# Gate weights split once and kept in HBM, norms and x scaling on ScalarE, rotary sum on GpSimd, the chunk loop written out

## The chip, the cores and the metric

The kernel runs on one core of one Trainium2 chip. The metric is the device time of one execution in microseconds (us). Five engines run their own instruction streams and meet at semaphores: TensorE (PE, its weight loads PEld), VectorE (DVE), ScalarE (ACT), GpSimd (POOL) and SyncE (SP), which here issues every DMA.

## The reference

One decoder layer on x of 2 x 1024 tokens, 256 wide, in float32:

```python
x = layernorm(x + mamba(x))       # rmsnorm, 1024-wide input projection, causal conv of 4 taps, silu,
                                  # selective scan with 16 states over 512 channels, gate, output projection
x = layernorm(x + xattn(x, ctx))  # two 8-head cross-attentions to the same 64 context tokens, rotary on
                                  # q and k, one softmax over 128 keys, W_o, layernorm, 256x256 layer, relu
x = layernorm(x + moe(x))         # 8 experts, top 2 of a softmax gate, plus a shared one; each is
                                  # (silu(x@w1+b1) * (x@w3+b3)) @ w2 + b2
# rotary: t * cos + rotate_half(t) * sin
```

The kernel computes all 9 expert networks for all tokens and weighs them. For w1 and w3 it splits weights and activations in a rounded part (hi) and a remainder (lo), so that three fast products (hi*hi, hi*lo, lo*hi) give the precision of float32.

## The kernel before, in words

**Tiling.** The 2048 tokens are four chunks of 512, two for each sequence. A chunk passes a first part, the mixer (rmsnorm, projections, conv, scan, output projection, first layernorm), and a second part (attention, layer norms, experts).

**Stages.** The second part of chunk j runs beside the mixer of chunk j+1. `body(i)` issues the mixer of chunk i and the second part of chunk i-1. body(0) has a mixer alone, bodies 1 to 3 have both and are a hardware loop (`Fori`), and body(4) has a second part alone; bodies 0 and 4 are written out already. So five stretches follow one another: a scan alone, three times scan and second part together, and a second part alone.

**What sets the order.** A list of steps written by hand, `schedule()`. Every engine walks the same list and issues its own share of each step, in order. The scan has 35 steps s; each holds, in this order: `early` work of the second part, the state sums (DVE, L1103, two), `mid` work of the second part, the scan step (DVE, L1051, two scans; ACT, L627, the two exponentials of the next step; POOL, L531, one product dbu of 128x1024 for the next step), and `late` work. dbu has a ring of three buffers, so POOL may be some steps ahead. The second part has its own counter of such steps, t = s + 2; below, "step" means one of these.

- t = 1 to 3, the rotation: q is computed on PE in four PSUM banks, ACT copies it with its bias to SBUF (L650), SP swaps neighbouring partitions by DMA, POOL multiplies the swapped copy by sin (L548, two of 128x1024), DVE multiplies by cos (L1193, two) and adds (L1198, two). PE's scores (L836) wait for both sums, and DVE's maximum of the scores (L1203) stands one step later.
- t = 14 and 15, the inner layernorm `xl`; t = 17 and 18, the layernorm `x2`. DVE makes mean and variance (`deviations`), POOL the power -0.5 of the variance (L537), DVE applies both (L1129, four of 128x256), then PE transposes. `x1` after the mixer and `xo` at the end go the same way.
- t = 20 to 39, the experts, 18 halves c. For each half SP loads 256 KB of w1 and w3 (L427), ACT rounds them to w_hi (L693), POOL makes w_lo (L555). PE multiplies (L862, six for the gate rows a and six for b), ACT makes two halves of the silu (L706, L708), POOL multiplies one by the expert's weight (L563, 16 of 18 halves), DVE multiplies them (L1219, two SBUF inputs) and takes in b (L1225, one input from PSUM), and PE applies w2 (L939). This is done for each of the four chunks, so 72 times.
- At s = 23 to 26 the next chunk is fetched: SP loads it into xn, ACT squares it, DVE and POOL make the rms, and DVE scales it (L1014, four of 128x256). The loop does so in body 3 too, for a chunk that does not exist; it loads chunk 0 again and nobody uses it.

## Time and profile before

| what | us |
|---|---|
| median of 3 runs | 1235.49 |
| the three runs | 1227.16, 1235.49, 1241.56 |
| span of the profiled execution | 1224.7 |

Apart from the span nothing is recorded of the profiled execution's own time; the three runs lie 2.5 to 16.9 us over its span.

| engine | busy us | share of the span |
|---|---|---|
| PE | 929.7 | 76% |
| PEld | 700.9 | 57% |
| DVE | 922.6 | 75% |
| POOL | 528.2 | 43% |
| ACT | 489.6 | 40% |

An average over unlike stretches says little, so the stretches are read one by one: busy time by engine in each, then the chain of waits inside it. Times in rows are us from the start of the span; L12 is line 12 of the kernel before.

### The profile page before, as it was taken

The page shows a single profiled execution, that of the slowest core. Times are in us where ns is not written, and L with a number is a line of the kernel's source. Part 1 is how long each engine was busy: PE and PEld are TensorE (multiplying, and loading weights), DVE is VectorE, ACT ScalarE, POOL GpSimd, SP SyncE. Part 2 cuts the span into 40 slices and gives each one's busy share as a digit, 9 for nine tenths or more (in the row PEclk, how much of TensorE's full clock was granted, in tenths as well). Part 3 has the DMA queues.
Part 4 walks back from the last instruction along what each step waited for, and adds up shares of the span by engine and source line. Part 5 has one row for each costly group of instructions (what it writes and reads, how often), then busy time and mean ns, then how long its engine had stood idle before and what let it go on. Part 6 is the DMA issues. An engine that isn't in the chain of part 4 may idle for free.

```text
span 1224.7 us, 13783 instructions
## 1 busy us (share of the span) xinstructions
PE 929.7 (76%) x3960; PEld 700.9 (57%) x3960; DVE 922.6 (75%) x1323; ACT 489.6 (40%) x911; POOL 528.2 (43%) x311
## 2 busy tenths in 40 slices
PE   4845549668689899577689899486789896677996
PEld 2434435256468685165477785165468683554885
DVE  2699996589999966689999965789789965322233
ACT  3534423544246434454345424454245421211442
POOL 1266540453457740533367730544257741001553
PEclk9855558778669999678679899678579997665999
DMA  5100101201023211101023211201023212000331
GB/s 193 36 35 35 52 1 35 70 35 61 18 70 121 77 45 54 70 35 61 18 78 127 73 36 55 85 18 61 18 72 119 86 35 91 21 1 9 117 109 42
DMA packets 38254, 72.61 MB, mean 59 GB/s; under 512 B 3871, under 2 KB 12712, under 8 KB 38174
## 3 DMA queue, kind: packets, MB, share of 16 engines
q1 hardware_dynamic: 38174, 71.65, 17.8%
q8 instruction: 37, 0.61, 0.2%
q14 instruction: 43, 0.35, 0.1%
HBM read 65.14 MB, written 2.30 MB: 55 GB/s over the span
## 4 chain that ended last, share of the span: by engine, by line
PE 45%; DVE 23%; issue 20%; POOL 6%; ACT 3%; DVEq 1%; POOLq 0%; DMA 0%; ACTq 0%; SPq 0%
PE ps L862 11%; DVE hs L1051 7%; PE ps L939 7%; PE ps L718 6%; PE ps L797 5%; POOL dbu L531 4%; DVE yacc L1103 4%; PE ps L836 3%; PE ps L791 2%; PE ps L825 2%; DVE work L1219 2%; PE ps L881 2%; PE ps L776 2%; DVE xn L1014 1%; POOL work L563 1%
## 5 line engine op out<-in xcount | busy, mean ns | idle before, releaser
L531 POOL TENSOR_TENSOR dbu<-v,bbc 128x1024 f32<-128x1024 f32 x128 | 308.9, 2418 | 257.3 <-DVE hs L1051 136.3
L1051 DVE TENSOR_TENSOR_SCAN hs<-ps,carry,dbu 128x512 f32<-128x512 f32 x256 | 313.3, 1266 | 10.1 <-ACT ps L627 8.2
L627 ACT ACTIVATE ps<-delta,neg_a 128x512 f32<-128x512 f32 x256 | 175.7, 692 | 300.5 <-DVE hs L1051 300.4
L718 PE MATMUL ps<-ident,hs 128*128 128x128 f32 x1024 | 189.1, 344 | 116.5 <-DVE yacc L1103 99.5
L718 PEld LDWEIGHTS ps<-ident,hs 128*128 128x128 f32 x1024 | 157.0, 180 | 150.0 <-DVE hs L1051 72.4
L1103 DVE SCALAR_TENSOR_TENSOR yacc<-ps,ctok,yacc 128x512 f32<-128x512 f32 x240 | 167.3, 737 | 1.2 <-PE ps L718 1.0
L555 POOL TENSOR_TENSOR w_lo<-w13s,w_hi 128x512 fp32r<-128x512 f32 x72 | 94.5, 1313 | 145.1 <-ACT w_hi L693 145.1
L939 PE MATMUL ps<-w2s,work 128*128 128x256 f32 x576 | 140.4, 388 | 0.3
L939 PEld LDWEIGHTS ps<-w2s,work 128*128 128x128 f32 x576 | 109.0, 196 | 15.9 <-DVE work L1225 1.5
L1219 DVE SCALAR_TENSOR_TENSOR work<-work 128x512 f32<-128x512 f32 x72 | 82.3, 1143 | 46.5 <-POOL work L563 45.6
L862 PE MATMUL ps<-x_hi,w_hi 128*128 128x512 f32 x288 | 107.9, 457 | 9.4 <-DVE work L1225 9.2
L706 ACT ACTIVATE work<-ps,half_b 128x512 f32<-128x512 f32 x72 | 49.5, 688 | 160.9 <-PE ps L862 151.3
L836 PE MATMUL ps<-kblk,work 128*128 (+1 forms) x128 | 47.5, 536 | 67.3 <-DVE work L1198 57.6
L563 POOL TENSOR_TENSOR work<-work,cbc 128x512 f32<-128x512 f32 x64 | 84.3, 1317 | 22.6 <-ACT work L706 22.6
L862 PE MATMUL ps<-x_hi,w_lo 128*128 128x512 f32 x288 | 93.6, 407 | 0.0
L862 PE MATMUL ps<-x_lo,w_hi 128*128 128x512 f32 x288 | 93.1, 406 | 0.0
L1225 DVE SCALAR_TENSOR_TENSOR work<-ps,vec,work 128x512 f32<-128x512 f32 x72 | 54.1, 751 | 46.2 <-PE ps L862 36.1
L836 PEld LDWEIGHTS ps<-kblk,work 128*128 128x128 f32 x128 | 33.2, 272 | 79.0 <-issue 62.9
L862 PEld LDWEIGHTS ps<-x_hi,w_hi 128*128 128x128 f32 x288 | 55.2, 199 | 22.8 <-DVE work L1225 12.3
L862 PEld LDWEIGHTS ps<-x_hi,w_lo 128*128 128x128 f32 x288 | 56.9, 198 | 13.2
L862 PEld LDWEIGHTS ps<-x_lo,w_hi 128*128 128x128 f32 x288 | 56.5, 196 | 13.1
L797 PE MATMUL ps<-yacc,win 128*128 128x512 f32 x128 | 57.7, 610 | 0.8 <-ACT yacc L592 0.8
(159 smaller groups left out, 1243.0 us busy)
## 6 DMA issues: line engine op xcount, KB each, us to landing
w13s<-in_w SPq DMA_DIRECT2D x72, 256.0 KB, 2.9
bbc<-brow_dram SPq DMA_DIRECT2D x32, 512.0 KB, 4.0
w2s<-in_w SPq DMA_DIRECT2D x36, 256.0 KB, 2.7
cbc<-comb_dram SPq DMA_DIRECT2D x32, 256.0 KB, 3.5
work<-work SPq DMA_DIRECT2D x16, 256.0 KB, 2.3
xn<-in_x SPq DMA_DIRECT2D x5, 512.0 KB, 5.3
xt<-in_x SPq DMA_DIRECT2D x4, 512.0 KB, 3.6
rope<-in_rope_q SPq DMA_DIRECT2D x4, 512.0 KB, 4.2
```

The costliest lines, as they stand in the source:

```text
L531: pool.tensor_tensor(dbu[:, i % DRING, :, :], v[:, 2 * h:2 * h + 2, :], bbc[:, n // 2 % 2, n % 2, :].rearrange("p (o t) -> p o t", o=1) .t ...
L555: pool.tensor_tensor(w13_lo[:, c % HRING, :, :, :].bitcast(F32R), w13s[:, c % HRING, :, :, :], w13_hi[:, c % HRING, :, :, :], ALU.subtract ...
L563: pool.tensor_tensor(gac[:, ib, :], ga[:, ib, :], cbc[:, g % CRING, :], ALU.mult).then_inc(gac_done.sem, 1)
L627: act.activation(ps[:, unit % 2, :], delta[:, q, :], ACT.Exp, scale=neg_a[:, q * NS + m:q * NS + m + 1]).then_inc(da_done.sem, 1)
L718: last = pe.transpose(ps[:, bank, t * P:(t + 1) * P], src(t), ident[:, :])
L797: last = pe.matmul(ps[:, m % Q, :], win[:, k, m * P:(m + 1) * P], xnt[:, k, :], start=(k == 0), stop=(k == KD - 1))
L836: last = pe.matmul(ps[:, 4 + b // 2, b % 2 * 2 * KEYS:(b % 2 + 1) * 2 * KEYS], qr[:, b, tile * P:(tile + 1) * P], kblk[:, bass.ds(j // CPS ...
L862: last = pe.matmul(o, left(l, k).bitcast(F32R), right(r, k).bitcast(F32R), start=(i == 0 and k == 0), stop=(i == len(terms) - 1 and k == K ...
L939: last = pe.matmul(out_cols(tile), hh[:, ib, tile * P:(tile + 1) * P], w2s[:, e % WRING, ib * DM:(ib + 1) * DM], start=False, stop=(c == 2 ...
L1051: dve.tensor_tensor_scan(hs[:, m % 2, q, 0:TC], ps[:, unit % 2, :], dbu[:, n % DRING, q % 2, :], carry[:, m, q:q + 1], ALU.mult, ALU.add). ...
L1103: dve.scalar_tensor_tensor(out=yacc[:, t, :], in0=ps[:, 2 + t % 2, :], scalar=c, in1=yacc[:, t, :], op0=ALU.mult, op1=ALU.add).then_inc(y_ ...
L1219: dve.scalar_tensor_tensor(out=gm[:, ib, :], in0=th[:, ib, :], scalar=1.0, in1=(gac if c >= 2 else ga)[:, ib, :], op0=ALU.add, op1=ALU.mul ...
```

## The change

- Gate weights. In body(0) alone, at steps s = 8 to 25, the 18 halves are staged in SBUF (SP, ring of 4, 256 KB each), rounded (ACT) and subtracted (POOL), and hi and lo are stored together in an HBM tensor (SP, 512 KB each). Each expert half of each chunk then loads hi and lo at once, 512 KB, and nothing is computed on them. The load of half c waits for the b products of half c-3; before it waited for w_lo of half c-3.
- Norms. ACT applies the four layernorms as x * rstd + shift; DVE makes -mean (128x4) and POOL shift = -mean * rstd (128x4), one small instruction each more. ACT also scales xn.
- Rotation. DVE reads q from PSUM, adds the bias and multiplies by cos in one instruction for each of 4 banks (128x512). POOL adds the two products after its two sin products.
- The loop over bodies 1 to 3 is written out, and the unused fetch in body 3 is gone.

```diff
@@ schedule
         steps += [("early", t), ("sum", s), ("mid", t), ("scan", s), ("late", t)]
+        if s >= 8:
+            steps.append(("split", s - 8))
@@ buffers
-        w13s = sb("w13s", [P, HRING, 2, KD, P])
-        w13_hi = sb("w13_hi", [P, HRING, 2, KD, P])
-        w13_lo = sb("w13_lo", [P, HRING, 2, KD, P])
+        w13x = sb("w13x", [P, HRING, 2, 2, KD, P])
+        w13_hi, w13_lo = w13x[:, :, 0, :, :, :], w13x[:, :, 1, :, :, :]
...
+        stage = work[:, 3072:5120].rearrange("p (a n) -> p a n", a=SRING)
+        w13_dram = nc.dram_tensor("w13_dram", (2 * ALL, P, 4 * KD * P), F32, kind="Internal").ap()
@@ streams
-            body(0, True, False)
-            with eng.Fori(1, CHUNKS, 1) as i:
-                body(i, False, False)
-            body(CHUNKS, False, True)
+            for i in range(CHUNKS + 1):
+                body(i, i == 0, i == CHUNKS)
@@ SP
+            def stage_half(c):
+                if c >= SRING:
+                    sp.wait_ge(lo_done.sem, c - SRING + 1)
+                sp.dma_start(stage[:, c % SRING, :], w13[c]).then_inc(stage_in[c % SRING].sem, 16)
+            def split(c):
+                if c == 0:
+                    sp.wait_ge(setup_pe.sem, 2)
+                    for k in range(SRING):
+                        stage_half(k)
+                if 1 <= c <= 2 * ALL:
+                    sp.wait_ge(lo_done.sem, c)
+                    sp.dma_start(w13_dram[c - 1], w13x[...]).then_inc(w13_out[(c - 1) % HRING].sem, 16)
+                    if c - 1 + SRING < 2 * ALL:
+                        stage_half(c - 1 + SRING)
             def load_half(j, c):
-                if c >= HRING:
-                    sp.wait_ge(*lo_done.at(j, c - HRING + 1))
-                else:
-                    sp.wait_ge(*lo_done.at(j, 0))
-                sp.dma_start(w13s[:, c % HRING, ...], w13[c]).then_inc(w13_in[c % HRING].sem, 16)
+                if j == 0 and c < HRING:
+                    for s in range(HRING):
+                        sp.wait_ge(w13_out[s].sem, 16 * (2 * ALL // HRING))
+                sp.wait_ge(*b_ps.at(j, max(0, c - HRING + 1)))
+                sp.dma_start(w13x[:, c % HRING, ...], w13_dram[c]).then_inc(w13_in[c % HRING].sem, 16)
...
-                c = t - T_EXP + 1 + HRING
+                c = t - T_EXP - 1 + HRING
                 if HRING <= c < 2 * ALL:
                     load_half(j, c)
@@ POOL
+                if kind == "split" and n < 2 * ALL:
+                    pool.wait_ge(hi_done.sem, n + 1)
+                    pool.tensor_tensor(w13_lo[:, n % HRING, ...], stage[:, n % SRING, :], w13_hi[:, n % HRING, ...],
+                                       ALU.subtract).then_inc(lo_done.sem, 1)
...
             def rstd_of(j, k):
...
+                pool.wait_ge(*norm[k]["rstd"].at(j, 1))
+                pool.tensor_tensor(shift[k][:, :], minus[k][:, :], rstd[k][:, :], ALU.mult
+                                   ).then_inc(norm[k]["shift"].sem, 1)
...
+                        for s in range(2):
+                            b = slice(2 * s, 2 * s + 2)
+                            pool.wait_ge(*sin_done.at(j, s + 1))
+                            pool.wait_ge(*cos_done.at(j, 2 * s + 2))
+                            pool.tensor_tensor(qr[:, b, :], qr[:, b, :], qs[:, b, :], ALU.add).then_inc(q_done.sem, 1)
...
-                    c = t - T_EXP + 1
-                    if 0 <= c < 2 * ALL:
-                        pool.wait_ge(*hi_done.at(j, c + 1))
-                        pool.tensor_tensor(w13_lo[:, c % HRING, ...], w13s[:, c % HRING, ...],
-                                           w13_hi[:, c % HRING, ...], ALU.subtract).then_inc(lo_done.sem, 1)
@@ ACT
+                if kind == "fetch" and n == 3:
+                    act.wait_ge(*rms_done.at(j, 1))
+                    for t in range(NT):
+                        last = act.activation(xn[:, t, :], xn[:, t, :], ACT.Copy, scale=rms[:, t:t + 1])
+                    last.then_inc(xn_done.sem, 1)
+                if kind == "split" and n < 2 * ALL:
+                    act.wait_ge(stage_in[n % SRING].sem, 16 * (n // SRING + 1))
+                    if n >= HRING:
+                        act.wait_ge(w13_out[n % HRING].sem, 16 * (n // HRING))
+                    act.activation(w13_hi[:, n % HRING, ...], stage[:, n % SRING, :], ACT.Copy).then_inc(hi_done.sem, 1)
...
+            def normalise(j, k, src, dst, after):
+                act.wait_ge(*norm[k]["shift"].at(j, 1))
+                for t in range(NT):
+                    act.activation(dst[:, t, :], src[:, t, :], ACT.Identity, scale=rstd[k][:, t:t + 1],
+                                   bias=shift[k][:, t:t + 1]).then_inc(after.sem, 1)
@@ PE
-                    pe.wait_ge(*lo_done.at(j, c + 1))
+                    pe.wait_ge(*w13_in[c % HRING].at(j, 16 * (c // HRING + 1)))
@@ DVE
                 dve.tensor_scalar(ve[k][:, :], mean[:, :, 1], EPS, None, ALU.add).then_inc(norm[k]["ve"].sem, 1)
+                dve.tensor_scalar(minus[k][:, :], mean[:, :, 0], -1.0, None, ALU.mult).then_inc(norm[k]["ve"].sem, 1)
...
                 if t == T_ROT:
-                    for s in range(2):
...
-                        dve.tensor_tensor(qr[:, b, :], qr[:, b, :], rope_part(0), ALU.mult).then_inc(cos_done.sem, 1)
-                    for s in range(2):
...
-                        dve.tensor_tensor(qr[:, b, :], qr[:, b, :], qs[:, b, :], ALU.add).then_inc(q_done.sem, 1)
+                    dve.wait_ge(*rope_in.at(j, 16))
+                    for b in range(HB):
+                        dve.wait_ge(*qs_in[b // 2].at(j, 32))
+                        dve.scalar_tensor_tensor(out=qr[:, b, :], in0=ps[:, 4 + b, :], scalar=col("bq", b),
+                                                 in1=rope[:, 0, :], op0=ALU.add, op1=ALU.mult).then_inc(cos_done.sem, 1)
```

GpSimd in body(0), at s = 8 and after. Before, 27 products dbu stand in a row:

```order
L510 MEMSET vx 128x528
L531 TENSOR_TENSOR dbu<-v,bbc 128x1024 x27
L515 TENSOR_TENSOR rms<-ms,power 128x4
L531 TENSOR_TENSOR dbu<-v,bbc 128x1024 x5
```

Now:

```order
L535 MEMSET vx 128x528
L561 TENSOR_TENSOR dbu<-v,bbc 128x1024 x10
L548 TENSOR_TENSOR w13x<-work,w13x 128x512
L561 TENSOR_TENSOR dbu<-v,bbc 128x1024
L548 TENSOR_TENSOR w13x<-work,w13x 128x512
L561 TENSOR_TENSOR dbu<-v,bbc 128x1024
```

From the tenth on, each dbu has one remainder (L548, `stage` is part of `work`) ahead of the next.

VectorE in body(1), at the rotation and the two steps after it. Before:

```order
L1193 TENSOR_TENSOR work<-work,rope 128x1024 x2
L1196 ISA
L1198 TENSOR_TENSOR work<-work 128x1024
L1196 REGISTER_ALU
L1198 TENSOR_TENSOR work<-work 128x1024
...
L1203 TENSOR_REDUCE mx<-ps 128x8
```

Now, in one piece (L1099 is the scan, L1227 the cos product):

```order
L1099 SCALAR_TENSOR_TENSOR hs<-ps,carry,dbu 128x512 x2
L1227 SCALAR_TENSOR_TENSOR work<-ps,vec,rope 128x512 x4
L1099 SCALAR_TENSOR_TENSOR hs<-ps,carry,dbu 128x512 x2
L1233 TENSOR_REDUCE mx<-ps 128x8
```

The sums have left VectorE. They stand on GpSimd now, ahead of the dbu of the third scan step (L581 is sin, L587 the sum):

```order
L561 TENSOR_TENSOR dbu<-v,bbc 128x1024 x2
L581 TENSOR_TENSOR work<-work,rope 128x1024 x2
L587 TENSOR_TENSOR work<-work 128x1024 x2
L561 TENSOR_TENSOR dbu<-v,bbc 128x1024 x11
```

## Rows read from the trace of the kernel before

**Rows 1.** Stages: us, busy us of each engine (instructions), clock share, DMA share, GB/s.
```profile
62.80:182.00 119.20, 58.25 (x240) 47.07 (x240) 119.20 (x130) 46.62 (x86) 69.14 (x30) 0.50 0.09 31
508.90:616.00 107.10, 68.41 (x345) 54.94 (x345) 101.10 (x126) 42.98 (x91) 49.05 (x22) 0.74 0.11 36
616.00:731.00 115.00, 105.64 (x507) 88.67 (x507) 102.50 (x129) 51.78 (x97) 74.10 (x47) 0.92 0.25 81
1129.60:1210.00 80.40, 79.72 (x348) 65.66 (x349) 27.53 (x59) 33.57 (x54) 41.30 (x32) 0.98 0.31 95
```

**Rows 2.** Timeline, scan alone: start us, us, engine, line, [idle before <- releaser].
```profile
95.53 1.38 DVE L1103 SCALAR_TENSOR_TENSOR yacc<-ps,ctok,yacc 128x512 f32<-128x512 f32 x2
95.65 0.69 ACT L627 ACTIVATE ps<-delta,neg_a 128x512 f32<-128x512 f32 x1 [0.48 <-DVE hs L1051]
95.76 2.35 POOL L531 TENSOR_TENSOR dbu<-v,bbc 128x1024 f32<-128x1024 f32 x1 [1.31 <-DVE hs L1051]
96.83 2.45 DVE L1051 TENSOR_TENSOR_SCAN hs<-ps,carry,dbu 128x512 f32<-128x512 f32 x2
...
99.20 1.38 DVE L1103 SCALAR_TENSOR_TENSOR yacc<-ps,ctok,yacc 128x512 f32<-128x512 f32 x2
...
157.94 5.13 DVE L1014 TENSOR_SCALAR xn<-xn,rms 128x256 f32<-128x256 f32 x4
```

**Rows 3.** Timeline, the rotation of the second overlapped stretch.
```profile
508.32 4.64 POOL L548 TENSOR_TENSOR work<-work,rope 128x1024 f32<-128x1024 f32 x2
...
511.29 6.02 DVE L1193 TENSOR_TENSOR work<-work,rope 128x1024 f32<-128x1024 f32 x2
...
517.24 4.49 DVE L1198 TENSOR_TENSOR work<-work 128x1024 f32<-128x1024 f32 x2
...
521.92 3.78 PE L836 MATMUL ps<-kblk,work 128*128 x8 [15.86 <-DVE work L1198]
```

**Rows 4.** Timeline, VectorE at the norms of that stretch.
```profile
583.13 5.01 DVE L1129 TENSOR_SCALAR xa<-xa,mv_xl,rstd_xl 128x256 f32<-128x256 f32 x4
...
596.82 0.76 DVE L1177 SCALAR_TENSOR_TENSOR x<-ps,x 128x256 f32<-128x256 f32 x2 [1.34 <-PE ps L907]
...
604.13 3.27 DVE L1129 TENSOR_SCALAR x<-x,mv_x,rstd_x 128x256 f32<-128x256 f32 x4
```

**Rows 5.** Timeline, TensorE among the experts of the first overlapped stretch.
```profile
388.69 0.81 PE L862 MATMUL ps<-x_hi,w_hi 128*128 128x512 f32 x2
...
394.04 0.81 PE L862 MATMUL ps<-x_hi,w_hi 128*128 128x512 f32 x2
```

**Rows 6.** Waits of TensorE, 385 to 415 us: us in total, times, longest.
```profile
PE ps L718 <- DVE yacc L1103: 3.4, 1, 3.4
PE ps L862 <- DVE work L1225: 3.3, 2, 1.7
```

**Rows 7.** Page, costliest groups: count | busy us, mean ns | idle before, releaser.
```profile
L555 POOL TENSOR_TENSOR w_lo<-w13s,w_hi 128x512 fp32r<-128x512 f32 x72 | 94.5, 1313 | 145.1 <-ACT w_hi L693 145.1
L1219 DVE SCALAR_TENSOR_TENSOR work<-work 128x512 f32<-128x512 f32 x72 | 82.3, 1143 | 46.5 <-POOL work L563 45.6
L1225 DVE SCALAR_TENSOR_TENSOR work<-ps,vec,work 128x512 f32<-128x512 f32 x72 | 54.1, 751 | 46.2 <-PE ps L862 36.1
```

**Rows 8.** One line each: duration ns as min/median/max.
```profile
L1219 DVE SCALAR_TENSOR_TENSOR work<-work x72: 658/693/2858, 357.2 to 1209.7; 128x512 f32<-128x512 f32 x72
```

**Rows 9.** DMA issues: count, KB each, median us from issue to landing.
```profile
bbc<-brow_dram SPq DMA_DIRECT2D x32, 512.0 KB, 4.0
...
wout<-in_w_out SPq DMA_DIRECT2D x1, 512.0 KB, 7.5
```

**Rows 10.** Stage with the most DMA traffic, columns as in rows 1.
```profile
0.00:30.00 30.00, 12.06 (x27) 6.08 (x28) 7.74 (x18) 9.47 (x21) 4.54 (x19) 1.00 0.58 197
```

**Rows 11.** Timeline of TensorE at the loop's back edge, and the tail.
```profile
464.25 1.09 PE L718 MATMUL ps<-ident,xn 128*128 128x128 f32 x8 [1.83 <-issue]
...
1099.35 1.01 POOL L537 TENSOR_TENSOR rstd_xl<-ve_xl,power 128x4 f32<-128x4 f32 x1 [56.65 <-DVE ve_xl L1123]
```

99 lines of the change are left out of this document (43 added, 56 removed).

## The prediction

> **What bounds the kernel now.** I read the busy times stage by stage first [rows 1]. In the scan alone VectorE is busy for all of 119.2 us and TensorE for half: VectorE is the bound. In the second overlapped stretch up to the experts, VectorE is busy 101.1 of 107.1 us. Among its experts TensorE is busy 105.6 of 115.0 and VectorE 102.5: the bound passes between them. The last 80 us, experts without a scan, are TensorE's alone (79.7 of 80.4). GpSimd and ScalarE are at 65% or less everywhere.
>
> Then the timeline of one scan step [rows 2]: two sums from 95.53, two scans from 96.83, the next sums at 99.20. A step is 3.67 us, 1.30 + 2.37, without a gap. One dbu of 2.35 us stands beside it on GpSimd, which then waits for its ring. Next the places where VectorE does something else: the scaling of xn [rows 2], the rotation [rows 3], the norms [rows 4], the experts [rows 5 to 8].
>
> In all of them VectorE instructions are longer than their size asks. L1219 takes 658 ns at best and 2858 at worst [rows 8], a span of one dbu. Four products of 128x256 of xn take 5.13 us [rows 2], though a scan over 128x512 takes 1.22. What suffers has all its inputs in SBUF; the sums and scans, which read PSUM, take the same time everywhere. So an instruction that leaves VectorE gives back its waiting too, where VectorE is late.
>
> **The change part by part.** The sum is made against the span, 1224.7 us; the median of the runs lies 10.8 above it, and I add that at the end.
>
> *Scaling of xn, in the scan alone:* 5.13 us leave the engine that bounds [rows 2]. ScalarE does it in four instructions of at most 0.69 (the exponential, twice as wide [rows 2]), between two exponentials that have over 1 us of slack. **-5.0**. In the other three bodies it falls among the experts, below.
>
> *The split, in the scan alone:* 18 steps get a w_hi, a w_lo, one load and one store. VectorE gets nothing, but its scans wait for dbu, which now stands behind w_lo, and that behind w_hi and the exponentials. From the end of a scan pair: exponential 0.69, w_hi at most 0.69 (same width), w_lo 1.31 [rows 7], dbu 2.35: 5.04. VectorE reaches the scan that reads this dbu after sums, a pair and sums, 4.97. So the cover is just used up: 0 to 0.1 a step, **+1**. SP stores a half one step after it is made, and w_hi needs the buffer three steps (11 us) later; its loads are issued four halves ahead. The other bound is DMA rate: 768 KB a step and the usual 512 KB in four steps are 0.92 MB. At 197 GB/s, the most this trace moves [rows 10], that is 4.7 us for a step of 3.7, +18 in all. I take +1, since the engines are only 58% busy at 197 GB/s.
>
> *Rotation, three overlapped bodies:* today two cos products 6.02 and two sums 4.49 keep VectorE from 511.3 to 521.7, and the scores start at 521.92 [rows 3]. Afterwards: four instructions of the form of L1225, 0.75 each [rows 7], done by 514.3; the sums on GpSimd run from 512.9, where the sin products end, for 2 x 2.32 (half of the 4.64 of the sin products [rows 3]), to 517.6. The scores start there. VectorE does its next scan pair meanwhile, but then stands before the maximum of the scores and waits for GpSimd and TensorE, so its own 7.5 us do not all count: -4.3, and as much in the other two, **-12.7**. The next dbu waits behind the sums, ends near 520, and its scan comes after the scores: hidden.
>
> Here a rule speaks against the change. The rows show products on GpSimd of 2.32 us beside a quiet VectorE, and VectorE's sum of the same size at 2.25 beside a busy GpSimd. The Trainium skill, GPSIMD Engine Reference, Engine selection, says to put elementwise sums of two inputs on VectorE, GpSimd being about twice as slow. The trace agrees only where VectorE is left alone. The skill's Perfetto Trace Analysis, Optimizing Scalar/DVE Operations, adds that moving work between the two "might not help" because of a shared SBUF port; that would make this term about 3 instead of 12.7, and it is rival C.
>
> *Inner norm xl, three bodies:* 5.01 us leave VectorE [rows 4]. TensorE's transposes wait for it; ScalarE has it done 1.4 us after its exponentials, some 4.2 earlier than today. VectorE already waits 1.34 us for the layer behind it at 596.8, so the gain is that of the chain: **-12.6**.
>
> *Norm x2, three bodies:* 3.27 us [rows 4], less the new small instruction and a short wait for x_hi, 2.9: **-8.7**. The norms x1 and xo stand inside the bodies where TensorE runs the projections without waiting for them: 0.
>
> *Experts, three bodies:* TensorE's step is 5.35 us where nothing holds it (394.04 - 388.69 [rows 5]). It loses 6.7 us to VectorE in the first stretch [rows 6], 6.0 and 6.7 in the others. VectorE's step without collisions is 1.30 + 2.37 + 0.66 + 0.75 = 5.08, below 5.35. With xn gone and GpSimd's load per step down from 5.0 to 3.7 us (w_lo, 72 times 1.31 [rows 7]), it should keep up. Collisions of L1219 with dbu remain possible, so I count 5.5 of each: **-16.4**. Bounds: 10.2 (only the wait behind xn, 3 x 3.4) and 19.4 (all). ScalarE's w_hi was hidden: 0.
>
> *Loads of 512 KB, 72 times:* hidden. The load of half c starts after the b products of half c-3, 2.8 us into a step, and the half is wanted two steps on: 7.9 us beside a scan, 6.2 in the tail. A 512 KB load lands in 4.0, in the crowded start in 7.5 [rows 9].
>
> *Loop:* TensorE stands 1.83 us at each of two back edges [rows 11]: **-3.7**. The unused fetch in body 3 is in the experts' term.
>
> *Tail:* four norms each get a multiplication on GpSimd and one on VectorE ahead of them, with everything waiting. No row shows the first; it lies between nothing and the power's 1.01 us [rows 11]. I take 0.3 and 0.1, as the power is most likely slow for what it computes: +1.6. The rotation there has no scan beside it; the sums are slower on GpSimd: +1.1, between -4 and +2.3. **+2.7**.
>
> Sum: -5.0 + 1 - 12.7 - 12.6 - 8.7 - 16.4 - 3.7 + 2.7 = -55.4. Span 1169.3, with 10.8 a time of **1180**.
>
> **The rivals.**
>
> A. *The expert loads become the bound (slower).* Place: every expert step. The step is at least (issue and landing + 2.8)/2. At 7.5 us of landing, 0.3 of issue, it is 5.3: hidden beside a scan, +15 in the tail. For the whole kernel to be over 12 us slower, the 54 steps at 5.35 and 18 at 4.48 must lose 67 together, a step of 6.06, so a landing of 9.0 us: about 1248. Against: 4.0 for the same size [rows 9], and 0.9 MB a step is below what 0 to 30 us moved [rows 10]. 4%.
>
> B. *The split throttles the first scan*, by DMA rate as worked out above: +17 against my term, 1197. For it: DMA traffic there rises from 31 GB/s to some 250. 12%.
>
> C. *GpSimd gives nothing back.* If its sums take 3.3 us each under VectorE's lock (6.6 for two dbu was seen), the scores come only 1 us earlier in three bodies: +9.7, 1190. This is what the second page above would have. For: GpSimd and VectorE do hold each other up. Against: the new cos products read PSUM, and such forms do not collide. 8%.
>
> D. *L1219 meets dbu in every step.* With w_lo gone GpSimd runs dbu right behind L563, and L1219 waits 2.2 us for it each time: VectorE's step is 7.3, +1.9 in some 42 steps, 1259, slower. It decides from 85% of the steps on; today the mean delay is about 0.8. A late VectorE shifts its L1219 past the dbu, so it does not lock. 2%.
>
> E. *More comes back.* VectorE is rid of some 93 us in all (60 of norms and xn, 29 of rotation, the rest collisions); if nearly the whole overlapped part is its bound, 1158. 10%.
>
> The forecast itself has 60%, with 1168 to 1193 around it for the unknown sizes; the last 4% are for mixtures of A and B that end near no change. Within 1% of 1235 (12 us) is what runs of this kernel cannot tell from none. That gives faster 0.90, same 0.04, slower 0.06. The range from **1156 to 1203** takes in the forecast, B, C and most of E, and leaves out A, D and the mixtures.
>
> **What would show it.** In the profile after: in the scan alone steps of 3.7 to 3.8 us through the split, and no stop of 5 us; dbu idle short, ended by w_lo's line. At the rotation, scores about 4 us earlier after the first scan pair, with VectorE waiting for PE ahead of the maximum. No scaling or norm rows on VectorE. Among the experts TensorE steps at 5.35 throughout and no waits for L1225 or the sums at the xn step. TensorE waiting for the w13x load would be A. L1219 near 2.8 us in the median would be D. ScalarE's norms ending later than the exponentials can bear, with scans waiting for L674, would make me wrong in a way I have priced at nothing.

## The result, and the profile after

| | median us | runs |
|---|---|---|
| before | 1238.53 | 1227.16, 1241.56, 1235.49, 1243.16 |
| changed | 1153.2 | 1155.19, 1151.21, 1150.85, 1156.8 |

The ratio is 0.9364, with a 95% interval from 0.932 to 0.9408: 85 us less. Faster was forecast at 0.90, and 1180; the time lies 27 below that and 3 below the range, next to rival E (1158). By the ratio, on the 1235.49 from which the forecast was made, it is 1156.9, at the range's lower edge. Every ratio in this document leaves out runs more than 1.5% above the quickest of their kernel, which for the kernel with the loop alone (below) are seven of ten, while the medians take in all runs. The profiled execution took 1155.19 us, its span is 1153.4, so here 1.8 lies around the span.

The engines' busy time on the page after:

```profile
PE 894.8 (78%) x3960; PEld 681.1 (59%) x3960; DVE 812.2 (70%) x1254; ACT 490.4 (43%) x929; POOL 475.0 (41%) x280
```

VectorE is rid of 110 us of work, GpSimd of 53 in spite of its new sums; ScalarE has as much as before, other things. The stages that answer [rows 1], with the same columns:

```profile
61.00:180.00 119.00, 59.01 (x244) 47.88 (x245) 117.42 (x128) 57.77 (x108) 91.04 (x48) 0.50 0.43 150
476.00:577.50 101.50, 69.07 (x349) 54.67 (x348) 86.70 (x120) 48.56 (x100) 56.74 (x28) 0.76 0.15 52
577.50:683.10 105.60, 98.53 (x503) 83.63 (x503) 89.09 (x126) 44.24 (x86) 52.46 (x29) 0.95 0.41 128
1050.00:1140.00 90.00, 88.06 (x377) 72.62 (x376) 28.65 (x62) 24.25 (x40) 20.41 (x16) 0.92 0.43 132
```

Beside the experts VectorE has gone from 102.5 of 115.0 us to 89.1 of 105.6: TensorE alone is the bound there now. Up to the experts VectorE is busy 86.7 of 101.5 us, where it was busy nearly throughout. Only the scan alone is still VectorE's.

To see where the 71 us between the spans went, I took TensorE's first instruction of each kind as a landmark and summed the way from one to the next over the three overlapped stretches. All kernels that the experiments below profiled are read with the same marks. "Gate products" are TensorE's products with w1 and w3, where the experts begin.

| us, three bodies together | before | changed | difference | forecast |
|---|---|---|---|---|
| start, to the end of the first projections | 35.9 | 34.6 | -1.2 | 0 |
| scan alone | 151.2 | 149.5 | -1.7 | -4 |
| y transposes to scores (rotation, two back edges) | 206.8 | 187.8 | -19.0 | -16.4 |
| scores to transposes of the inner norm (attention, xl) | 200.1 | 196.8 | -3.3 | -12.6 |
| those to the transposes of x2 (layer, x2) | 63.5 | 49.2 | -14.3 | -8.7 |
| those to the first gate products | 25.4 | 17.6 | -7.8 | 0 |
| gate products, first to last (experts) | 340.2 | 313.0 | -27.2 | -16.4 |
| tail, from the last gate product beside a scan to the end | 217.1 | 220.4 | +3.3 | +2.7 |

(The experts overlap the next y transposes by 7.8 us, twice, in both kernels. Less these 15.5 the rows add up to the two spans.)

**The split in the scan alone.** Timeline, with scans, exponentials, w_hi (L631), w_lo (L548) and dbu (L561); it answers [rows 2]:

```profile
93.39 2.35 POOL L561 TENSOR_TENSOR dbu<-v,bbc 128x1024 f32<-128x1024 f32 x1
...
95.05 0.62 ACT L631 ACTIVATE w13x<-work 128x512 fp32r<-128x512 f32 x1
...
95.74 1.27 POOL L548 TENSOR_TENSOR w13x<-work,w13x 128x512 fp32r<-128x512 f32 x1
95.84 2.46 DVE L1099 TENSOR_TENSOR_SCAN hs<-ps,carry,dbu 128x512 f32<-128x512 f32 x2 [0.15 <-issue]
96.97 2.35 POOL L561 TENSOR_TENSOR dbu<-v,bbc 128x1024 f32<-128x1024 f32 x1
...
99.51 2.45 DVE L1099 TENSOR_TENSOR_SCAN hs<-ps,carry,dbu 128x512 f32<-128x512 f32 x2
```

GpSimd goes dbu, w_lo, dbu without a rest, and each dbu ends (95.74, 99.32) some 0.1 to 0.2 us before the scan that reads it: a scan pair comes every 3.67 and 3.91 us by turns, 3.79 on average for 3.67 before.

**The rotation**, second overlapped stretch, answering [rows 3]:

```profile
480.38 4.65 POOL L581 TENSOR_TENSOR work<-work,rope 128x1024 f32<-128x1024 f32 x2
480.67 2.46 DVE L1099 TENSOR_TENSOR_SCAN hs<-ps,carry,dbu 128x512 f32<-128x512 f32 x2 [2.72 <-issue]
483.04 2.70 DVE L1227 SCALAR_TENSOR_TENSOR work<-ps,vec,rope 128x512 f32<-128x512 f32 x4
484.99 4.64 POOL L587 TENSOR_TENSOR work<-work 128x1024 f32<-128x1024 f32 x2
...
489.68 3.78 PE L890 MATMUL ps<-kblk,work 128*128 128x256 f32 x8 [11.83 <-POOL work L587]
493.50 1.23 DVE L1233 TENSOR_REDUCE mx<-ps 128x8 f32<-128x1024 f32 x1 [5.39 <-PE ps L890]
494.76 1.80 DVE L1236 TENSOR_SCALAR top<-mx 128x8 f32<-128x8 f32 x1
```

The scores start 9.3 us after the sin products; before, it was 13.6 (521.92 - 508.32). The new cos products take 2.70 for four, the sums 2.32 each, and VectorE waits 5.39 for TensorE ahead of the maximum, all as forecast. The last row is a thing I had not looked at: `top` has eight numbers a partition and takes 1.80 us.

**The experts**, groups of the page that answer [rows 7], and the distribution that answers [rows 8]:

```profile
L1249 DVE SCALAR_TENSOR_TENSOR work<-work 128x512 f32<-128x512 f32 x72 | 54.6, 758 | 1.2 <-ACT work L762 0.9
L1255 DVE SCALAR_TENSOR_TENSOR work<-ps,vec,work 128x512 f32<-128x512 f32 x72 | 54.1, 751 | 105.6 <-PE ps L916 85.5
```
```profile
L1249 DVE SCALAR_TENSOR_TENSOR work<-work x72: 661/682/1656, 340.7 to 1137.4; 128x512 f32<-128x512 f32 x72
```

The product gm (L1249, formerly L1219) falls from a mean of 1143 ns to 758, from a longest of 2858 to 1656, and VectorE's idle time before it from 46.5 us to 1.2. Before, 29 of the 54 gm of the three overlapped stretches began while a dbu was running; now 2 do. TensorE, which had waited 6.7 us for VectorE in 30 us [rows 6], waits for nothing at the same place (364 to 394 us).

**Loads** ([rows 9]): 512 KB of split weights land in 3.4 us, and no expert step waits for them.

```profile
w13x<-w_dram SPq DMA_DIRECT2D x72, 512.0 KB, 3.4
```

### The profile page after: what moved, and what is told of

Same layout as the page of the kernel before. It is cut to its first block, busy times and chain, and to the rows that moved or that the text cites. A ratio compares the mean times of both kernels' runs of the same rounds, so it can differ in the third digit from the quotient of the medians.

```text
span 1153.4 us, 12464 instructions
## 1 busy us (share of the span) xinstructions
PE 894.8 (78%) x3960; PEld 681.1 (59%) x3960; DVE 812.2 (70%) x1254; ACT 490.4 (43%) x929; POOL 475.0 (41%) x280
## 4 chain that ended last, share of the span: by engine, by line
PE 57%; DVE 17%; POOL 10%; issue 9%; ACT 5%; DVEq 0%; DMA 0%; POOLq 0%; ACTq 0%; SPq 0%
PE ps L916 17%; PE ps L993 10%; PE ps L772 8%; PE ps L851 5%; DVE hs L1099 5%; POOL dbu L561 5%; PE ps L890 3%; PE ps L879 3%; DVE yacc L1149 3%; POOL w13x L548 2%; PE ps L960 2%; DVE mx L1233 2%; PE ps L830 1%; ACT work L725 1%; PE ps L845 1%
## 5 line engine op out<-in xcount | busy, mean ns | idle before, releaser
L561 POOL TENSOR_TENSOR dbu<-v,bbc 128x1024 f32<-128x1024 f32 x128 | 304.1, 2385 | 213.3 <-DVE v L1085 112.3
L1099 DVE TENSOR_TENSOR_SCAN hs<-ps,carry,dbu 128x512 f32<-128x512 f32 x256 | 313.3, 1265 | 8.2 <-issue 8.0
L772 PE MATMUL ps<-ident,hs 128*128 128x128 f32 x1024 | 180.3, 333 | 93.8 <-DVE yacc L1149 78.9
L916 PE MATMUL ps<-x_hi,w13x 128*128 128x512 f32 x576 | 175.5, 428 | 0.0
L596 POOL TENSOR_TENSOR work<-work,cbc 128x512 f32<-128x512 f32 x64 | 86.7, 1355 | 203.8 <-ACT work L760 154.3
L760 ACT ACTIVATE work<-ps,half_b 128x512 f32<-128x512 f32 x72 | 49.6, 689 | 211.9 <-PE ps L916 211.9
L1255 DVE SCALAR_TENSOR_TENSOR work<-ps,vec,work 128x512 f32<-128x512 f32 x72 | 54.1, 751 | 105.6 <-PE ps L916 85.5
L916 PEld LDWEIGHTS ps<-x_hi,w13x 128*128 128x128 f32 x576 | 112.0, 197 | 24.1 <-issue 1.7
L890 PE MATMUL ps<-kblk,work 128*128 128x256 f32 x128 | 45.0, 513 | 61.3 <-POOL work L587 47.6
L916 PE MATMUL ps<-x_lo,w13x 128*128 128x512 f32 x288 | 92.2, 402 | 0.0
L916 PEld LDWEIGHTS ps<-x_lo,w13x 128*128 128x128 f32 x288 | 56.2, 195 | 12.8
L725 ACT ACTIVATE work<-ps,top 128x128 f32<-128x128 f32 x128 | 34.8, 384 | 67.4 <-DVE top L1236 67.4
L1249 DVE SCALAR_TENSOR_TENSOR work<-work 128x512 f32<-128x512 f32 x72 | 54.6, 758 | 1.2 <-ACT work L762 0.9
L1233 DVE TENSOR_REDUCE mx<-ps 128x8 f32<-128x1024 f32 x16 | 19.5, 1216 | 49.2 <-PE ps L890 49.2
L762 ACT ACTIVATE work<-ps,half_b 128x512 f32<-128x512 f32 x72 | 49.0, 681 | 0.0
```

What stands on the lines that cost most here:

```text
L561: pool.tensor_tensor(dbu[:, i % DRING, :, :], v[:, 2 * h:2 * h + 2, :], bbc[:, n // 2 % 2, n % 2, :].rearrange("p (o t) -> p o t", o=1) .t ...
L596: pool.tensor_tensor(gac[:, ib, :], ga[:, ib, :], cbc[:, g % CRING, :], ALU.mult).then_inc(gac_done.sem, 1)
L772: last = pe.transpose(ps[:, bank, t * P:(t + 1) * P], src(t), ident[:, :])
L890: last = pe.matmul(ps[:, 4 + b // 2, b % 2 * 2 * KEYS:(b % 2 + 1) * 2 * KEYS], qr[:, b, tile * P:(tile + 1) * P], kblk[:, bass.ds(j // CPS ...
L916: last = pe.matmul(o, left(l, k).bitcast(F32R), right(r, k).bitcast(F32R), start=(i == 0 and k == 0), stop=(i == len(terms) - 1 and k == K ...
L1099: dve.tensor_tensor_scan(hs[:, m % 2, q, 0:TC], ps[:, unit % 2, :], dbu[:, n % DRING, q % 2, :], carry[:, m, q:q + 1], ALU.mult, ALU.add). ...
```

## Experiments

Times are medians. Each kernel has its ratio to the kernel before on its own chip; 0.01 is 12 us. For the kernel with the loop alone I go by the ratio. The edits are shown abridged, partly in words.

| kernel | us | ratio (95%) | gm ns | top ns |
|---|---|---|---|---|
| changed | 1153.2 | 0.9364 (0.932 to 0.9408) | 758 | 973 |
| changed, weights as before | 1163.9 | 0.9467 (0.9433 to 0.9501) | 1134 | 918 |
| changed, xn on VectorE | 1167.0 | 0.948 (0.9446 to 0.9513) | 741 | 972 |
| changed, norms on VectorE | 1190.3 | 0.9679 (0.9634 to 0.9725) | 758 | 878 |
| changed, rotation as before | 1159.1 | 0.9434 (0.9397 to 0.9471) | 758 | 599 |
| changed, x2 alone on VectorE | 1163.0 | 0.9488 (0.9397 to 0.9578) | 759 | 871 |
| before, loop written out | 1223.2 | 0.9834 (0.9743 to 0.9926) | 1151 | 610 |
| before, loop written out, and the split | 1211.7 | 0.9798 (0.964 to 0.9955) | 742 | 711 |
| before, loop written out, and the norms | 1189.0 | 0.9698 (0.9627 to 0.9768) | 1144 | 508 |
| norms on VectorE, TensorE kept busy | 1193.1 | 0.9752 (0.9662 to 0.9842) | 758 | 905 |
| changed, split thinned, tail | 1146.2 | 0.9328 (0.9247 to 0.941) | 759 | 961 |
| changed, w_lo later, tail | 1142.7 | 0.9334 (0.9254 to 0.9415) | 758 | 937 |
| the last, and thinned | 1144.7 | 0.9346 (0.9272 to 0.9419) | 758 | 848 |

**1. Weights as before.** The inverse of the change's lines for the split:

```
-                steps.append(("split", s - 8))
-                sp.dma_start(w13x[...], w13_dram[c])
+                sp.dma_start(w13s[...], w13[c])
+ act:  w_hi of half c = t - T_EXP + 1, early
+ pool: w_lo of the same half, early, ahead of dbu
```

> The changed kernel with its gate weights handled as before: each chunk loads the raw half (256 KB), ScalarE makes w_hi and GpSimd w_lo in every expert step; the split in the scan alone is gone, all else is as in the changed kernel. The changed kernel lies at 1153.2 us, its expert stretches beside a scan at 104.3 each. Theory 1 (the w_lo in front of dbu is what makes dbu fall on L1249): VectorE's gm comes back to a mean of 1.0 us or more (0.76 in the changed kernel), each expert stretch to 109 to 112, the way from the x2 transposes to the first gate matmul takes some 2 us more in each body, and the scan alone becomes 2 to 4 us shorter: together +18 to +28, a time of 1171 to 1181. Theory 2 (VectorE has room now that the scaling of xn and the rest are off it, and w_lo fits): gm stays under 0.85 us, expert stretches stay within 1 us, and the time is 1150 to 1158, with nothing but the shorter scan alone to be seen.

Measured: 1163.9, +10.7, between the two theories. The mechanism is the first one's:

```profile
L1227 DVE SCALAR_TENSOR_TENSOR work<-work 128x512 f32<-128x512 f32 x72 | 81.7, 1134 | 45.7 <-POOL work L575 36.3 <-issue 8.3 <-ACT work L740 0.9
```

gm is back at 1134 ns with 45.7 us of idle time before it, and the experts take 325.9 for 313.0 (108.8, 110.2 and 106.9). Of the 54 gm beside a scan 34 begin under a running dbu again. The scan alone is 3.5 shorter, 146.0: that is the price of the split, and I had it at 1. The way from x2 to the gates did not lengthen, so that part of my first theory is wrong.

**2. Scaling of xn on VectorE.**

```
+ dve: dve.tensor_scalar(xn[:, t, :], xn[:, t, :], rms[:, t:t + 1], None, ALU.mult)
- act: act.activation(xn[:, t, :], xn[:, t, :], ACT.Copy, scale=rms[:, t:t + 1])
```

> The changed kernel with the scaling of xn back on VectorE (four products of 128x256 a chunk), all else as changed. Theory 1 (VectorE is the bound wherever a scan runs, and what stands in its row counts in full): +4 to +5 in the scan alone, +3 to +4 in each of three expert stretches, in all +13 to +17, a time of 1166 to 1170. Theory 2 (beside the experts VectorE has 0.27 us of slack a step, and the experts' step of 5.35 on TensorE absorbs one late step within the ring): +4 to +5 in the scan alone and at most 1 in each expert stretch, 1157 to 1161.

Measured: 1167.0, +13.8, in the first theory's range. 6.0 of it is in the scan alone, and 1.1, 1.9 and 2.1 in the experts, half of what I expected there; the rest is spread over stretches that moved by 1 to 3 us either way. gm stays at 741 ns: the collisions have nothing to do with xn.

**3. All norms on VectorE.**

```
+ dve: dve.tensor_scalar(dst[:, t, :], src[:, t, :], mean[:, t, 0:1], rstd[k][:, t:t + 1],
+                        ALU.subtract, ALU.mult)
- act: act.activation(dst[:, t, :], src[:, t, :], ACT.Identity, scale=rstd[k][...], bias=shift[k][...])
```

> The changed kernel with all four norms applied on VectorE again (and without the negated mean and the shift), all else as changed. By the terms of the prediction, xl 4.2 and x2 2.9 in each of three bodies, less 1.6 in the tail: +20, a time of 1173. The landmarks of the changed kernel showed nothing from scores to the transposes of the inner norm in two bodies of three: if the chain of the attention tiles and not VectorE's row sets that stretch, xl gives 0 to 2 us a body and the whole is +8 to +13, 1161 to 1166.

Measured: 1190.3, +37, nearly twice the prediction's term and three times my rival. Attention to the inner transposes: +10.2; those to x2's: +20.7; those to the gates: +7.8; tail -3.9. (The two profiled executions are 32.8 us apart.) Timeline of the second overlapped stretch, this kernel:

```profile
582.08 4.69 POOL L561 TENSOR_TENSOR dbu<-v,bbc 128x1024 f32<-128x1024 f32 x2
582.27 5.30 DVE L1160 TENSOR_SCALAR x<-x,mv_x,rstd_x 128x256 f32<-128x256 f32 x4
587.49 2.45 DVE L1082 TENSOR_TENSOR_SCAN hs<-ps,carry,dbu 128x512 f32<-128x512 f32 x2
587.63 1.97 PE L755 MATMUL ps<-ident,x 128*128 128x128 f32 x8 [4.04 <-DVE x L1160]
...
589.86 1.38 DVE L1134 SCALAR_TENSOR_TENSOR yacc<-ps,ctok,yacc 128x512 f32<-128x512 f32 x2
...
591.31 1.29 DVE L1201 TENSOR_TENSOR x_lo<-ps,x_hi 128x512 fp32r<-128x512 f32 x2
```

and the same place in the changed kernel, which answers the last of [rows 4]:

```profile
570.03 2.45 DVE L1099 TENSOR_TENSOR_SCAN hs<-ps,carry,dbu 128x512 f32<-128x512 f32 x2
570.12 6.99 POOL L561 TENSOR_TENSOR dbu<-v,bbc 128x1024 f32<-128x1024 f32 x3
570.20 2.08 ACT L684 ACTIVATE x<-x,shift_x,rstd_x 128x256 f32<-128x256 f32 x4 [3.68 <-POOL shift_x L570]
...
572.33 1.97 PE L772 MATMUL ps<-ident,x 128*128 128x128 f32 x8 [0.79 <-ACT x L684]
572.40 1.38 DVE L1149 SCALAR_TENSOR_TENSOR yacc<-ps,ctok,yacc 128x512 f32<-128x512 f32 x2
...
574.12 0.69 DVE L1206 TENSOR_TENSOR x_lo<-ps,x_hi 128x512 fp32r<-128x512 f32 x1 [0.34 <-ACT x_hi L747]
```

Two things are to be seen. On VectorE the norm takes 5.30 us under two dbu, on ScalarE 2.08 beside three. And behind the norm on VectorE stand a scan pair and two sums, 3.8 us, before x_lo, for which the gates wait; on ScalarE the same pair and sums run while the norm is applied, and x_lo follows the transposes by 1.8 us instead of 3.7. I had priced the first with the one row 3.27, and the second not at all.

**4. Rotation as before.**

```
+ dve: two cos products from SBUF, two sums          (6.0 + 4.5 us)
- dve: four cos products of 128x512 from PSUM
- pool: two sums
```

> The changed kernel with the rotation of the queries as before (two cos products from SBUF and two sums, all on VectorE), all else as changed. By the prediction's term: +4.3 in each of three bodies, -1.1 in the tail: +12, a time of 1165. The landmarks gave 3.5 to 6.1 a body, so up to +17, 1170. The rival: VectorE's next scans absorb it, since they have caught up by the maximum of the scores: under +6, 1159 or less.

Measured: 1159.1, +5.9, at the rival. But up to the scores it loses 3.8, 3.2 and 5.0, 12.0 together, which is the prediction's 12.7. Attention then gives 6.0 back (190.8 us for 196.8). Part of it is `top`: 599 ns on average here, 973 with the sums on GpSimd. The next row of the changed kernel shows why.

```profile
513.74 2.35 POOL L561 TENSOR_TENSOR dbu<-v,bbc 128x1024 f32<-128x1024 f32 x1 [1.31 <-DVE hs L1099]
514.74 1.37 DVE L1236 TENSOR_SCALAR top<-mx 128x8 f32<-128x8 f32 x1
```

`top` has its input in SBUF and ends when the dbu beside it ends. The four kernels of the table with the rotation on VectorE have `top` at 508 to 711 ns (the kernel before: 648), the nine with the sums on GpSimd at 848 to 973. Over the kernel that is 15.6 us for 9.6 here, as much as the attention gives back. That all of it lies on the path is argued, not shown: by bodies the attention moved by +1.7, -3.2 and -4.5, and the granted clock moves such a stretch too.

**5. x2 alone on VectorE.** As 3, for x2 only.

> The changed kernel with the norm x2 alone back on VectorE; xl, x1 and xo stay on ScalarE. With all four norms back the time was 1190.3, 37 more than the changed kernel, and the landmarks put 5.0 to 10.4 of it between the inner norm's transposes and those of x2, and 1.6 to 3.3 between these and the first gate matmul, in each of three bodies. Theory 1 (order: on VectorE the four products, which wait for a dbu and so take 5.2 instead of 3.3, stand ahead of a scan pair of 2.45; moved away, that pair runs while ScalarE applies the norm, and x_lo follows the transposes at once, instead of behind the pair): +7 to +9 a body, less 1 in the tail, so +20 to +26, 1173 to 1179. Theory 2 (only the products themselves count, as the prediction had it): +2.9 a body, +8, 1161, and the rest of the 37 belongs to xl.

Measured: 1163.0, +9.8, below the first theory and near the second. The stretches say otherwise: +9.3 up to x2's transposes, +7.8 from there to the gates, 17.1, or 5.7 a body; attention (-4.4), experts (-2.4) and tail (-2.9) give more than half of it back. Of the 2.9 in the tail, 1.0 is the norm, which is slower on ScalarE there; for the rest I have no cause shown. So both theories miss: the cost at its place is nearer to the first, what it costs in the end is the second's.

**6. Before, with the loop written out.**

```
-            with eng.Fori(1, CHUNKS, 1) as i:
-                body(i, False, False)
+            for i in range(CHUNKS + 1): body(i, i == 0, i == CHUNKS)
```

> The kernel before with its loop over the chunks written out, and nothing else of the change but that the unused fetch of a fifth chunk goes. The kernel before lay at 1231.5 beside the last four. Theory 1: the two back edges (1.83 us each on TensorE) and the unused scaling among the last experts (3.4) go, -7, 1222 to 1227. Theory 2: the engines beside the one that waits at the back edge use the time, so that VectorE, which is the bound there, loses nothing by it: -3 or less, 1228 to 1232.

Measured: ratio 0.9834, some 20 us with an interval from 9 to 32: more than either theory. By the medians of all runs (1223.2 for 1232.4) it is 9 us, and 1223.2 lies in the first theory's range. In its profile the third body's experts take 105.0 us for 113.2, the other two 112.8 and 112.9 as before. That body had fetched a chunk that does not exist; without it 8 us go, where I had counted 3.4 (and that inside the term of the experts). The way to the scores is 3.1 shorter, the two back edges. The tail is 6.6 shorter here; it is the attention of the last chunk (50.1 us for 56.9), and it lies at 50.2 to 57.0 in kernels with the same code there, and no run shows why.

**7. The same, with the split.**

> The kernel before with the loop written out and the gate weights split once through HBM; norms, scaling of xn and rotation stay on VectorE. Compared with the one that has the loop alone. Theory 1 (w_lo pushes dbu onto gm, whatever else VectorE has to do): gm's mean falls from 1.14 to 0.76, -4 to -5 in each expert stretch, +3.5 in the scan alone, +2 in the tail: 7 to 9 less than the loop alone. Theory 2 (as long as VectorE is late its gm meets a dbu anyway, and only the whole set of moves frees it): gm's mean stays over 1.0, and the time is the same as or up to 5 more than the loop alone.

Measured: ratio 0.9798, 4 us less than with the loop alone, the intervals overlap. gm's mean falls to 742 ns with everything else still on VectorE, and the experts from 330.7 to 312.6; the scan alone costs 4.2. So w_lo is what had pushed dbu onto gm, and the second theory falls. But the gain is eaten elsewhere: the layer's stretch grew from 19.9 us to 26.7 in each body. The same place in the loop-only kernel, and in this one:

```profile
604.19 2.34 POOL L535 TENSOR_TENSOR dbu<-v,bbc 128x1024 f32<-128x1024 f32 x1
604.38 3.27 DVE L1133 TENSOR_SCALAR x<-x,mv_x,rstd_x 128x256 f32<-128x256 f32 x4
...
612.44 1.28 POOL L559 TENSOR_TENSOR w_lo<-w13s,w_hi 128x512 fp32r<-128x512 f32 x1 [5.90 <-ACT w_hi L697]
```
```profile
612.63 4.70 POOL L561 TENSOR_TENSOR dbu<-v,bbc 128x1024 f32<-128x1024 f32 x2
612.82 5.30 DVE L1155 TENSOR_SCALAR x<-x,mv_x,rstd_x 128x256 f32<-128x256 f32 x4
```

With w_lo in its queue GpSimd stood 5.90 us behind it and left the norm alone after one dbu. Without w_lo it runs two dbu on, and the norm takes 5.30 instead of 3.27. One part of the change makes another part's instruction costlier, 2.0 us a body, before that part takes it off VectorE.

The other 4.7 a body go with TensorE's granted clock. Windows of the layer's stretch, columns as in [rows 1]: loop alone, split added, norms on VectorE (second and third body), and the changed kernel.

```profile
587.75:607.71 19.96, 13.81 (x57) 9.46 (x57) 17.59 (x31) 5.64 (x9) 5.68 (x3) 0.76 0.09 27
```
```profile
591.49:618.17 26.68, 20.06 (x56) 12.99 (x56) 19.61 (x31) 5.64 (x9) 8.03 (x4) 0.50 0.06 20
```
```profile
566.22:587.63 21.41, 13.70 (x57) 9.52 (x57) 19.61 (x31) 5.65 (x9) 8.02 (x4) 0.74 0.06 24
830.57:857.25 26.68, 20.06 (x56) 12.99 (x56) 19.61 (x31) 5.64 (x9) 8.03 (x4) 0.50 0.06 20
```
```profile
556.09:572.33 16.24, 12.88 (x56) 9.11 (x57) 15.26 (x28) 7.61 (x14) 8.73 (x6) 0.82 0.11 34
```

The two middle ones are the same kernel, and VectorE's busy time in them is the same 19.61. Where the clock stays at half (0.50, 1.2 GHz) throughout, TensorE needs 20.06 us for what takes 13.70 at 0.74, and the stretch is 5.3 longer. Four products of the layer take 2.08 us at the one level and 1.13 at the other. The kernel before has this in its third body (24.6 us at 0.50, for 19.7 and 19.3). In the eight profiled kernels with x2 and xl on ScalarE, 24 bodies, the stretch is 16.2 to 16.7 us each time.

**8. Norms on VectorE, TensorE kept busy.** To test that the clock is the cause of the 20.7:

```
+                    for _ in range(12):
+                        pe.transpose(ps[:, 4, 0:P], ident[:, :], ident[:, :])
                     pe.wait_ge(*x2_done.at(j, NT))      # and so ahead of xl_done
```

> The changed kernel with all norms back on VectorE (the one that took 1190.3), and one thing more: ahead of the transposes of the inner norm and of x2 TensorE runs twelve transposes of the identity into a bank that is written over by the next instruction. They fall into the 3.7 and 4.0 us that TensorE stands there. Theory 1 (a standing TensorE is granted 1.2 GHz, and the layer and the gate products behind the wait run at it): the stretch between the two transposes, 21.4 to 26.7 at a mean granted clock of 0.73 to 0.50, falls to 18 to 20, the gate products behind x2 from 0.57 us a pair to 0.37, and the whole by 8 to 18 us, 1172 to 1182. Theory 2 (VectorE's row alone sets these stretches, the clock is a bystander): the same 1190, or up to 3 more for the transposes that are in the way.

Measured: 1193.1, no gain; my first theory falls. In the third body the mean clock rose to 0.84 and the stretch is as long as at 0.74; in the second it stayed low all the same:

```profile
578.70:605.40 26.70, 21.75 (x69) 14.85 (x69) 19.63 (x31) 5.64 (x9) 8.04 (x4) 0.55 0.06 20
840.84:862.28 21.44, 15.30 (x69) 11.38 (x69) 19.63 (x31) 5.65 (x9) 8.05 (x4) 0.84 0.08 24
```

So 21.4 is VectorE's row (19.6 busy), and no clock shortens it; the clock adds its 5.3 only where it stays at half through the layer. Of the 20.7 us that the norms cost between the two transposes, 15.4 (21.8, 21.4 and 21.4 less 49.2) is VectorE's row and 5.3 one such body. No run took the half clock away from such a body, so the 5.3 rest on the comparison of the two bodies. What makes the clock stay down in one and not in the next I could not show.

**9. Before, loop written out, with the norms on ScalarE.**

> The kernel before with the loop written out and the four norms applied on ScalarE; split, scaling of xn and rotation as before. Compared with the kernel before that has the written-out loop alone (1223, or 1203 in its quickest runs). Theory 1 (the norms give what they cost when they are put back, since the granted clock behind them comes with them): -25 to -37, 1186 to 1198. Theory 2 (the norms are worth what the prediction has for them, xl 4.2 and x2 2.9 in three bodies, and the rest of the 37 came from having all the other moves as well): -15 to -22, 1201 to 1208.

Measured: ratio 0.9698, 0.0136 below the loop alone: 17 us, give or take 14, and 18.9 between the two profiles. The time itself, 1189.0, lies in the first theory's range, and the two medians, from different chips, are 34 apart; the second theory is the nearer one by the ratio and by the profiles, but the interval does not exclude the first one's 25. Added to the old kernel the norms give about what the forecast had for them, 19.7 with the tail; put back in the new one they cost 32.8 between the profiles and 39, give or take 8, by the ratios. Over the three bodies alone it is 26.5 and 36.9. The longer row (2.0 a body) and the one body at half clock (5.3) are as much as the difference; the rest of the gap lies in the tail, which grew by 7.5 here, 3.4 of it in the last chunk's attention without a cause shown. In the old kernel the layer's stretch falls from 59.8 us only to 48.9, in the new one from 69.9 to 49.2. The attention stretch gains 8.7 (10.2 in the new one).

**10. A better version: split thinned, tail on VectorE.**

```
-        if s >= 8:
-            steps.append(("split", s - 8))
+        k, rest = divmod(2 * (s - 7), 3)
+        if s >= 7 and rest < 2:
+            steps.append(("split", k))
  # and for j == CHUNKS - 1: norms and rotation sums as before, on DVE
```

> The changed kernel with two edits: the split takes two scan steps of three instead of every one (it begins one step earlier and ends with the scan), and in the last chunk, which has no scan beside it, the norms and the rotation's sums are on VectorE as before. Theory 1: GpSimd's step in the split period is dbu 2.35 and w_lo 1.27, 3.62 and the semaphores between, against VectorE's 3.67; spread out it fits, -2.5 to -3.5 in the scan alone. The tail gives back the 1.0 at the first norm, 1.0 to 1.7 at the rotation, 1.0 at x2 and 1.0 at the last norm: -4. Together 1145 to 1147.5. Theory 2: the scan alone does not depend on how dense the splits are (each costs its 0.12 to 0.2 where it stands): only the tail's -4, 1149 to 1150.

Measured: 1146.2, as the first theory has it, but not for its reason. The scan alone is 149.1, so thinning gave 0.4. The tail gives back 1.0 at each of three norms (x1, x2, the last) and 3.6 at the rotation, but in all 5.1, since its attention and its experts moved by +3.7 and -2.0. The row that explains the scan:

```profile
96.44 1.26 POOL L549 TENSOR_TENSOR w13x<-work,w13x 128x512 fp32r<-128x512 f32 x1 [1.61 <-ACT w13x L635]
97.67 2.36 POOL L562 TENSOR_TENSOR dbu<-v,bbc 128x1024 f32<-128x1024 f32 x1
```

GpSimd, which may be some dbu ahead, stands 1.61 us until ScalarE has made w_hi, and its lead is gone.

**11 and 12. w_lo one split step later**, in every scan step, and in two of three.

```
+                if kind == "split" and 1 <= n <= 2 * ALL:
+                    c = n - 1
+                    pool.wait_ge(hi_done.sem, c + 1)
```

> The changed kernel with two edits: in the split GpSimd makes the w_lo of the half before, whose w_hi has been ready for a step, instead of the one of the same step; and the last chunk's norms and rotation sums are on VectorE. The split stands in every scan step, as in the changed kernel. In the run with the thinned split w_lo still began only when w_hi was made, 1.6 us after the last dbu had ended, and the scan alone took 149.1 (146.0 with no split at all). Theory 1 (the wait for w_hi is the cost, not the number of splits): the scan alone falls to 146 to 147, so the whole is 3 us below the thinned one, 1142 to 1144. Theory 2 (GpSimd's 3.62 us of work a step is itself the bound against VectorE's 3.67): 148 to 149.5, as it is.

> As the last, and the split besides in two scan steps of three. Theory 1 (the wait for w_hi was the cost): the scan alone at 146 to 147, the same as with the later w_lo alone. Theory 2 (density counts once the wait is gone): 146 to 147 here, 148 or more with the later w_lo alone. In both the time is 1142 to 1144.

Measured: 146.2 for the scan alone in both, what it takes with no split at all (146.0). The first theory is right: 18 splits are free once GpSimd does not wait for the w_hi of the same step. The timeline has scan pairs 3.67 and 3.66 apart:

```profile
92.22 2.45 DVE L1105 TENSOR_TENSOR_SCAN hs<-ps,carry,dbu 128x512 f32<-128x512 f32 x2
...
95.89 2.45 DVE L1105 TENSOR_TENSOR_SCAN hs<-ps,carry,dbu 128x512 f32<-128x512 f32 x2
...
99.55 2.45 DVE L1105 TENSOR_TENSOR_SCAN hs<-ps,carry,dbu 128x512 f32<-128x512 f32 x2
```

The first takes 1142.7 us, runs from 1140.3 to 1149.0, where the changed kernel's were 1150.9 to 1156.8. It is the quickest version seen; its ratio's interval overlaps the changed kernel's, and 3.3 us of the difference, in the scan alone, have their cause shown. Of the 11.5 us by which its profile's tail is shorter, 6.2 are the norms and the rotation's sums; the rest has no cause shown.

## Why the forecast was right in direction and too small

**The sum was 16 us short, and the 10.8 us on top did not hold.** The sum gave a span of 1169.3; it is 1153.4. By the table, x2 with the way to the gates brought 13.4 more than forecast and the experts 10.8 more; rotation, back edges and xl together brought 6.7 less, the scan alone 2.3 less. And the changed kernel's median lies 0.2 below its profiled span, not 10.8 above. The kernel before ran from 1217.8 to 1246.8 us over all chips here, at mean granted clocks from 0.808 down to 0.78; its profiled execution was a quick one. The changed kernel's four runs lie within 6 us, at 0.821 to 0.826. The runs show the spread and the clock together; I did not show that one makes the other.

Term by term:

- **xn in the scan alone, -5.0:** right; put back it costs 6.0.
- **Split, +1:** 3.5. My chain (5.04 against 4.97) had found the place, but took it for a matter of 0.1. What I left out is that GpSimd gives up its lead when it waits for the same step's w_hi. Rival B is ruled out: a 512 KB store lands in 2.9 us, and with the later w_lo the same traffic costs nothing.
- **Rotation, -12.7:** 12.0 by putting it back, the back edges apart. But the attention takes 6.0 of it, where `top` grew by as much. The prediction let the scans be the only thing behind it.
- **xl, -12.6:** 8.7 (added to the old kernel) to 10.2 (put back in the new one). It does not show in the table (-3.3) because the rotation's 6.0 stand in the same stretch. Two moves added and subtracted there.
- **x2, -8.7:** this step failed. It was costed by the length of one row and without what stands behind it on VectorE. At its place it is 17.1 in the new kernel: the row is 5.3 without w_lo, and scans and sums come between transposes and x_lo. 7.8 of it fell into a stretch for which I had forecast 0. The -14.3 of the table holds some luck besides: the third body of the kernel before had its layer at half clock, 24.6 us for 19.7 and 19.3, and without these 5 the row is near its forecast.
- **Experts, -16.4:** -27.2, beyond even the upper bound of 19.4, so this term failed too. I had counted only TensorE's waits for VectorE and put its own busy time at no change. For the same products it fell from 310.4 to 295.8 us, 14.6 in all, at a mean granted clock of 0.94 to 0.97 for 0.92 to 0.94 before; how much of it is the clock no run shows. By parts, the two things I named are there, the collisions and the wait behind xn (5.1 put back, half of the 10.2). Split: 18.1 added to the old kernel, 12.9 taken from the new. I had left "collisions remain possible" with GpSimd's load at 3.7 us a step; they are nearly gone, gm at 682 ns in the median. The unused fetch: 8.2, for 3.4.
- **Back edges, -3.7:** -3.1 in experiment 6.
- **Tail, +2.7:** +3.3, right by luck. The shift costs 0.20 us, not 0.3, but a norm on ScalarE takes 2.07 us for the 1.38 on VectorE with nothing beside it, so each of x1, x2 and the last comes out 1.0 later, not 0.4. The rotation costs 1.7 for 1.1 and the experts 2.1, and the last chunk's attention is 3.5 shorter, for which I have no cause shown.

**The rivals.** A: no expert step waits for a load that lands in 3.4 us. B: see above. C, that GpSimd would give nothing back: its sums take 2.32 us each and the scores come 12 us earlier; yet half of it was lost again in the attention, where dbu holds `top` up. The Trainium skill, Perfetto Trace Analysis, Optimizing Scalar/DVE Operations, says that moving work between the two might not help, for a port that they share. The trace disagrees at the place of the move, and agrees in part on the sum: 5.9 of 12.0 are left. One reading of mine behind this rival was wrong: VectorE's 2.25 us for a sum "beside a busy GpSimd" is the mean of two unlike ones, 3.36 begun under a dbu and 1.21 with nothing beside it. Alone VectorE is nearly twice as fast as GpSimd (1.21 for 2.34), but five of the eight sums took 3.36 and three 1.21:

```profile
L1198 DVE TENSOR_TENSOR work<-work x8: 1212/3354/3359, 243.3 to 1043.7; 128x1024 f32<-128x1024 f32 x8
```

D: gm was to meet dbu in every step once w_lo was gone; it begins under one in 2 of 54. E named 1158, close to the 1153.2, but in part by luck: its span was 1147, and it is 1153.4; E, too, had the 10.8 on top that did not come. Its reason, that what leaves VectorE comes back with its waiting, fits the rotation, the norms and gm; among the experts TensorE is the bound now.
